# Attention and mixture of experts over eight batches: a new first and last batch, and shorter expert sums on GpSimd

## What is computed

```
xn  = layernorm(x)
q, k, v = xn @ Wq.T, xn @ Wk.T, xn @ Wv.T
att = softmax((q @ k.T * tril) / sqrt(512)) @ v        # masked scores are 0, not -inf
g   = top 2 of softmax(xn @ Wg), normalised            # 8 experts
ffn = sum_e g[e] * (xn @ We[e] + be[e])
out = x + att + ffn
```

## Time and profile before

| what | us |
|---|---|
| median of 3 runs | 129.04 |
| lowest and highest run | 128.96, 131.56 |
| the profiled execution, its own time | 128.2 |
| its span in the trace | 126.4 |

### The profile page before, as it was taken

How to read it: one execution, slowest core, us unless ns; L and a number is a source line. 1 busy time by engine, 2 the same in 40 slices (tenths; PEclk the granted TensorE clock), 3 DMA queues, 4 the chain that set the end, 5 groups by cost and what they waited for, 6 DMA issues and landing times.

```text
span 126.4 us, 2983 instructions
## 1 busy us (share of the span) xinstructions
PE 117.3 (93%) x738; PEld 104.7 (83%) x738; DVE 111.4 (88%) x539; ACT 101.1 (80%) x339; POOL 92.5 (73%) x207
## 2 busy tenths in 40 slices
PE   4999589999999999999999999999999999999950
PEld 4877476998899988998999888998899889898940
DVE  0587998999999999999999999989999998979952
ACT  0746299989997999789987999799978999887620
POOL 7400338689977899699968997889869996858950
PEclk9999999999999999999999999999999999999996
DMA  3998000000200011000200020001100020000202
GB/s 96 295 313 210 1 3 5 0 3 3 83 0 5 3 39 44 0 0 8 83 3 0 0 83 5 3 3 37 48 0 0 5 83 0 3 0 15 76 0 83
DMA packets 9249, 5.18 MB, mean 41 GB/s; under 512 B 392, under 2 KB 9104, under 8 KB 9232
## 3 DMA queue, kind: packets, MB, share of 16 engines
q1 hardware_dynamic: 8656, 4.66, 13.4%
q10 hardware_dynamic: 576, 0.33, 0.9%
HBM read 2.89 MB, written 2.10 MB: 39 GB/s over the span
## 4 chain that ended last, share of the span: by engine, by line
PE 83%; DVE 7%; DMA 2%; issue 2%; ACT 1%; POOL 1%; ACTq 1%; DVEq 0%; POOLq 0%
PE attb L307 14%; PE ring L250 13%; PE ring L246 13%; PE ring L247 12%; PE score L291 7%; PE score L247 4%; PE score L250 4%; PE score L246 3%; PE ring L316 3%; DMA wqk_s<-in_w_attention_dram 2%; PE ring L326 2%; PE score L357 2%; PE attb L350 1%; PE ring L327 1%; PE ring L329 1%
## 5 line engine op out<-in xcount | busy, mean ns | idle before, releaser
L911 ACT ACTIVATE ysc<-ring,gate 128x128 f32<-128x128 f32 x124 | 35.3, 375 | 1.8 <-PE ring L250 1.8
L246 PE MATMUL ring<-w_hi,xT_hi 128*128 128x512 f32 (+2 forms) x96 | 34.7, 361 | 0.2 <-ACT xT_hi L992 0.2
L250 PE MATMUL ring<-w_hi,xT_lo 128*128 128x512 f32 (+2 forms) x96 | 32.7, 341 | 0.0
L247 PE MATMUL ring<-w_lo,xT_hi 128*128 128x512 f32 (+2 forms) x96 | 32.5, 338 | 0.0
L1099 POOL TENSOR_TENSOR ysc<-ysc 128x256 f32<-128x256 f32 x31 | 22.8, 737 | 8.6 <-ACT ysc L911 8.6
L307 PE MATMUL attb<-c_s,probT 128*128 128x128 f32 x160 | 23.6, 278 | 0.8 <-ACT probT L945 0.8
L307 PEld LDWEIGHTS attb<-c_s,probT 128*128 128x128 f32 x160 | 21.6, 192 | 2.2 <-ACT probT L945 1.1
L558 DVE SCALAR_TENSOR_TENSOR mix<-ring,gate,mix 128x128 f32<-128x128 f32 x64 | 21.9, 345 | 0.5
L246 PEld LDWEIGHTS ring<-w_hi,xT_hi 128*128 128x128 f32 x96 | 18.1, 189 | 2.8 <-ACT xT_hi L992 0.5
L930 ACT ACTIVATE prob<-score,nmx 128x128 f32<-128x128 f32 (+3 forms) x32 | 17.5, 550 | 2.5 <-DVE nmx L614 1.8
L247 PEld LDWEIGHTS ring<-w_lo,xT_hi 128*128 128x128 f32 x96 | 18.1, 189 | 1.7
(11 more groups left out here) (108 smaller groups left out, 255.6 us busy)
## 6 DMA issues: line engine op xcount, KB each, us to landing
x_all<-in_x_dram SPq DMA_DIRECT2D x7, 256.0 KB, 5.5
out_dram<-o_s SPq DMA_DIRECT2D x7, 256.0 KB, 2.4
w_f<-in_w_stacked_dram SPq DMA_DIRECT2D x1, 256.0 KB, 5.1
w_f<-in_w_stacked_dram SPq DMA_DIRECT2D x1, 192.0 KB, 3.8
w_f<-in_w_stacked_dram SPq DMA_DIRECT2D x1, 132.0 KB, 2.8
x_all<-in_x_dram ACTq DMA_DIRECT2D x1, 128.0 KB, 2.9
x_all<-in_x_dram SPq DMA_DIRECT2D x1, 128.0 KB, 2.6
wqk_s<-in_w_attention_dram ACTq DMA_DIRECT2D x1, 128.0 KB, 3.0
```

What stands on the lines that cost most here:

```text
L246: nc.tensor.matmul(dst, hi, w_h, start=True, stop=False)
L247: nc.tensor.matmul(dst, hi, w_l, start=False, stop=False)
L250: return nc.tensor.matmul(dst, lo, w_h, start=False, stop=True)
L911: last = nc.scalar.mul(ysc[:, t, e, :], bank(f"A{t}", b)[:, e * P:(e + 1) * P], gate[:, b % 2, t, e:e + 1])
```

## The change

Everything else than what follows is as before; batches 1 to 6 keep their order.

- First batch. `expert_biases`, `biases_hi` and VectorE's `bias_rhs` are gone. The host now lays the biases out over 128 rows (`be_rows`), one DMA of 64.5 KB brings them in place of two, and GpSimd makes the rows: a rounding copy, a multiplication by a column, four additions over 32 partitions each. The first `sv_rows` waits for them (`be_ready`).
- GpSimd also makes `w_lo` of piece A (128 x 512), after VectorE has normalised batch 0. ScalarE casts `w_hi` of piece A after `xT_hi` instead of ahead of it.
- VectorE takes the four statistics of batch 1 in one go ahead of `u_lo`.
- The products of the identity are 6 and 4 pairs instead of 5 and 6.
- SyncE issues the load of batch 1 (and, behind it, of batches 2 to 7) only when the weights of piece B have landed.
- TensorE, VectorE and ScalarE get new lists for the first and the last batch. In the last, ScalarE copies the transposed probabilities of tile 3 ahead of `rows_copy`, not behind it, and TensorE transposes them one product (A3) earlier.
- In all batches `sum_experts` takes three operations instead of four: y7 lies in a fourth slot of `mix`, and y7 and the B experts are added in one operation of 128 x 256. `scale_last_act` in the last batch now waits for all expert sums of the batch before.

```diff
-WARM = (5, 6)
+WARM = (6, 4)
...
             sp.dma_start(w_f[:, a_cols], w_stacked[:, a_cols]).then_inc(S["w_a"], 16)
+            sp.wait_ge(S["w_b"], 16)
             sp.dma_start(x_all[:, NT * P:2 * NT * P].rearrange("p (t d) -> p t d", d=P), x_v[1]).then_inc(S["x1"], 16)
...
                 if t == 0:
                     dve.wait_ge(S["svh_ready"], b + 1)
+                    if b == 0:
+
+                        dve.wait_ge(S["be_ready"], 1)
...
             def scale_last_act(b):
 
                 act.wait_ge(S["gate_ready"], b + 1)
-                act.wait_ge(S["ffn_ready"], (b - 2) * NT + NT)
+                act.wait_ge(S["ffn_ready"], b * NT)
...
                 chain.step(nc.gpsimd.tensor_tensor(y[:, 0:2, :], y[:, 0:2, :], y[:, 2:4, :], ALU.add))
-                chain.step(nc.gpsimd.tensor_tensor(y[:, 0, :], y[:, 0, :], y[:, 1, :], ALU.add))
                 pool.wait_ge(S["y7_ready"], b + 1)
-                chain.step(nc.gpsimd.tensor_tensor(y[:, 0, :], y[:, 0, :], y7[:, b % 2, t, :], ALU.add))
                 pool.wait_ge(S["mix_ready"], b * NT + t + 1)
+                chain.step(nc.gpsimd.tensor_tensor(y[:, 0:2, :], y[:, 0:2, :], mix[:, t, 2:4, :], ALU.add))
                 if b > 1:
                     pool.wait_ge(S["fin_done"], (b - 2) * NT + t + 1)
-                nc.gpsimd.tensor_tensor(ffn[:, b % 2, t, :], y[:, 0, :], mix[:, t, 2, :], ALU.add
+                nc.gpsimd.tensor_tensor(ffn[:, b % 2, t, :], y[:, 0, :], y[:, 1, :], ALU.add
                                         ).then_inc(S["ffn_ready"], 1)
...
+            def bias_rhs():
+
+                pool.wait_ge(S["w_be"], 16)
+                chain.step(nc.gpsimd.tensor_copy(be_hi[:], be_s[:, 0:P]))
+                chain.step(nc.gpsimd.tensor_scalar(be_hi[:].bitcast(F32), be_hi[:].bitcast(F32), be_s[:, P:P + 1], None, ALU.mult))
+                for t in range(NT):
+                    r = slice(t * ROWS, (t + 1) * ROWS)
+                    chain.step(nc.gpsimd.tensor_tensor(rhs_rows[r, t, :], be_s[r, 0:P], be_hi[r, :].bitcast(F32), ALU.add))
+                pool.sem_inc(S["be_ready"], 1)
...
-            chain.step(nc.gpsimd.memset(rhs_rows[:].bitcast(F32), 0.0))
-            pool.sem_inc(S["consts_ready"], 1)
+            nc.gpsimd.memset(rhs_rows[:].bitcast(F32), 0.0)
             normal_rstd(0)
+
+            pool.wait_ge(S["xn0_ready"], NT)
+            pool.wait_ge(S["wa_ready"], 1)
+            nc.gpsimd.tensor_tensor(w_lo[:, a_cols], w_f[:, a_cols], w_hi[:, a_cols].bitcast(F32), ALU.subtract
+                                    ).then_inc(S["wla_ready"], 1)
+            bias_rhs()
```

More of the change, by code:

```diff
@@ L79, in step, with build @@
         self.need(self.mark(instruction))
-def build(nc, x, w_attention, w_stacked, be, shapes, out):
+def build(nc, x, w_attention, w_stacked, be_rows, out):
     B, T, D = x.shape
-    E = be.shape[0]
+    E = (w_stacked.shape[1] - P) // (P + 1)
     NT = T // P
@@ L380, in _ @@
             wide(0, "C", 0)
-            expert_biases(0)
+            project_u(0)
             wide(0, "C", 1)
-            project_u(0)
             wide(0, "C", 2)
             wide(0, "C", 3)
-            value_sums(0)
             scores(0, 0)
             scores(0, 1)
+            value_sums(0)
+            wide(0, "B", 0)
+            wide(0, "A", 0)
+            transpose_probs(0, 0)
             scores(0, 2)
-            transpose_probs(0, 0)
-            wide(0, "A", 0)
-            wide(0, "B", 0)
+            scores(0, 3)
+            transpose_x(1)
+            attend(0, 0)
             wide(0, "A", 1)
-            attend(0, 0)
-            transpose_x(1)
-            scores(0, 3)
             wide(0, "B", 1)
             wide(1, "C", 0)
-            project_u(1)
             transpose_probs(0, 1)
             wide(1, "C", 1)
+            project_u(1)
             wide(1, "C", 2)
@@ L447, in _ @@
             transpose_rows(B - 2)
+            value_sums(B - 1)
             attend(B - 2, 3)
@@ L450, in _ @@
             bias(B - 2)
-            wide(B - 1, "A", 0)
             scores(B - 1, 2)
             wide(B - 1, "B", 0)
+            wide(B - 1, "A", 0)
             wide(B - 1, "A", 1)
+            scores(B - 1, 3)
             wide(B - 1, "B", 1)
-            scores(B - 1, 3)
             wide(B - 1, "B", 2)
@@ L459, in _ @@
             wide(B - 1, "A", 2)
+            transpose_probs(B - 1, 2)
+            wide(B - 1, "B", 3)
             attend(B - 1, 0)
-            wide(B - 1, "B", 3)
-            transpose_probs(B - 1, 2)
+            transpose_probs(B - 1, 3)
             wide(B - 1, "A", 3)
             attend(B - 1, 1)
-            transpose_probs(B - 1, 3)
             attend(B - 1, 2)
@@ L753, in _ @@
             mix_b(0, 0, 1)
+            mask_scores(0, 1)
             mix_b(0, 0, 2)
+            negate_max(0, 1)
             x_lo(1)
```

147 lines of the change are left out of this document (59 added, 88 removed).

## The result

| | before | changed |
|---|---|---|
| median (4 runs each, same chip) | 129.0 us | 125.19 us |
| lowest and highest | 128.7, 131.56 | 124.7, 125.94 |
| profiled execution, its span | 128.2, 126.4 | 125.6, 123.9 |

A forecast was written before the change was run, and what follows sets the result against it. TensorE, busy 14.00 of 14.00 us, was taken to bound the loop, leaving gains only at start and end. 1.7 + 0 + 0.84 = 2.5 us off 129.04 gave 126.5 us, range 125.6 to 128.2.

The forecast's parts named there:

- the start's gain: First batch: `normalize(1)` starts at 14.6 instead of 16.33, and the last product of the first list moves equally: 1.7 us.
- chain 1: First batch, GpSimd: transposes, casts, weight split until 10.0, bias rows until 13.2, `rstd` and `nmr` 1.29, `normalize(1)` at 14.6.
- T0: First batch: TensorE's first transposes, forecast to start at 6.75 us; 7.55 in the profile before.
- T0 to N: First batch: from the first transposes, forecast at 6.75, to the start of `normalize(1)`, forecast at 14.6.
- Chain 2: First batch, VectorE and ScalarE: exponential of tile 0 at 12.7, its transpose and copy until 14.0, 0.6 us to spare.
- Rival 3: First batch: GpSimd operations are cheap (under 0.3 each), so the VectorE and ScalarE chain decides; 125.9 us; chance 0.20.
- Rival 1: Start's gain given back: GpSimd's rows cost 0.82 each, or batch 1's load takes 5.5 us; 128.0 us; chance 0.20.
- Rival 4: First batch: seven x loads served side by side, batch 1 lands at 13.7, VectorE stands still; 130.4 us; chance 0.04.
- the rule that I had cited: Load of batch 1: DMA engines take a ring's descriptors in order, so it is in time; without this 1.3 us more.
- The loop: Batches 1 to 6: GpSimd's sum falls from 2.12 to 1.94 per tile, but TensorE waits for nothing, so worth 0.
- The end: Last batch: copying tile 3's probabilities ahead of `rows_copy` removes TensorE's wait of 0.84 us.
- rival 2: Last batch: ScalarE waits for batch 6's sums, tile 3's exponential comes over 0.8 late; 127.3 us; chance 0.16.

The follow-up runs named there:

- experiment 12: Changed kernel without SyncE's wait for weight piece B ahead of the load of batch 1: 125.01 us, ratio 0.9741.
- experiments 2 and 6: 2: changed kernel with the four-operation sum put back, 126.52 us, ratio 0.9877; 6: kernel before with the three-operation sums alone, 127.8 us, ratio 0.9949.
- experiment 9: Kernel before with four small VectorE operations per batch given one SBUF input instead of two (values differ): 129.0 us, ratio 0.9985.
- experiment 10: Kernel before with only the pair sums made a one-input reduction: 128.77 us, ratio 1.0.
- experiment 5: Changed kernel with only ScalarE's last two copies exchanged back, `rows_copy` ahead of tile 3's probabilities: 125.95 us, ratio 0.985.
- experiment 3: Changed kernel with the last batch's TensorE, VectorE and ScalarE lists of the kernel before, the wait for batch 6's sums kept: 125.61 us, ratio 0.9801.
- experiment 7: Changed kernel with VectorE's pair sums (128x3) moved behind `u_lo` in the first batch: 124.7 us, ratio 0.9763.
- the anchor: The changed kernel run once more, unaltered, against the kernel before: 124.66 us, ratio 0.9733.

## Why the prediction was right, and where it was not

**The place and the kind of the start's gain: right; its size in the profile: 0.72, not 1.7.** The chain was the one named: GpSimd, with VectorE's chain shorter. The terms of chain 1:

- T0 at 6.75 (forecast) came at 7.46. Four identity products fewer gave 0.86 between a and T0 (0.85 forecast). But a was 5.17 instead of 4.40, since the attention weights landed 3.8 us after their issue, not 3.0; that is the whole 0.77. Column a spreads like this in both codes (4.38 to 5.17 in ten profiles of changed kernels, 4.40 to 5.02 in four of before), so I take it for chance.
- T0 to N: forecast 14.6 - 6.75 = 7.85, measured 8.14 (8.06 to 8.20 in the eight profiles with this order). In the rows above it is 2.14 to the start of the split (forecast 2.05), 1.28 for the split (1.17), 3.32 for the bias rows until `rstd` starts (3.2), 1.40 for `rstd` and `nmr` (1.4). Three of the four terms were a little short, by 0.3 together.

With the landing of before, this step comes to 0.86 + 0.64 - 0.01 = 1.5 us. Chain 2 came out nearly right by luck: the exponential of tile 0 stood 6.10 behind T0 (forecast 5.95), although the small addition booked at 0.1 took 0.86; the other terms had been too large by 0.6 together. Rival 3 fell: the GpSimd operations were not cheap, though the copy alone was (0.28). Rival 1 fell too: the load of batch 1 was there for its first statistic, at 9.84. Rival 4 fell with it: the seven loads took 4.4 in the median, and experiment 12 shows that the wait moves nothing. Whether a ring is served in order, the rule that I had cited, no run here shows.

**The loop: wrong.** The step that failed is "TensorE waits for nothing there, so this is worth 0", on the row that gave TensorE 14.00 of 14.00 us. It was worth 0.86 between X1 and X7 (experiments 2 and 6). TensorE does pause, once per batch, ahead of `transpose_x`. Before:

```profile
71.77 0.34 PE L247 MATMUL score<-xT_lo,uT_hi 128*128 128x384 f32 x1
71.95 0.34 PE L250 MATMUL score<-xT_hi,uT_lo 128*128 128x384 f32 x1
72.24 0.63 PE L316 MATMUL ring<-ident,xn 128*128 128x128 f32 x4
72.70 0.27 PE L291 MATMUL score<-ident,prob 128*128 128x128 f32 x1
```

And in the changed kernel:

```profile
70.68 0.34 PE L247 MATMUL score<-xT_lo,uT_hi 128*128 128x384 f32 x1
70.85 0.34 PE L250 MATMUL score<-xT_hi,uT_lo 128*128 128x384 f32 x1
71.03 0.61 PE L313 MATMUL ring<-ident,xn 128*128 128x128 f32 x4
71.47 0.27 PE L291 MATMUL score<-ident,prob 128*128 128x128 f32 x1
```

The start after a product of this size comes 0.18 us later when nothing is missing (71.77 to 71.95); before, the transposes came 0.29 later. From one set of transposes to the next it was 13.22, 13.69, 13.60, 13.61, 13.62, 13.67 us before and is 13.26, 13.51, 13.41, 13.45, 13.44, 13.48 now: nothing gained in the first period, into which the new first list still reaches, and 0.16 to 0.19 in each of the other five. Of that the pause is 0.11 to 0.12, the transposes themselves 0.02; the rest is spread in hundredths. The modelled end of the product (0.34 from its start) covers the pause, and so the busy time reads full. The Trainium skill ("Perfetto Trace Analysis", "Identifying the Most-Contended Engine") says that matmul busy time is a poor measure of how near TensorE is to its limit, and names the busy share of the weight loads, beside the share of peak arithmetic, as a better one. The trace agrees: with 14.00 in both, the weight loads rose from 12.67 to 12.90. What would have shown the pause beforehand is the spacing of starts.

Behind the pause stands this chain. VectorE and GpSimd before:

```profile
67.05 0.38 DVE L624 TENSOR_TENSOR tot<-em,masked_keys 128x4 f32<-128x4 f32 x1
...
68.86 0.17 DVE L490 TENSOR_SCALAR veps<-mv 128x4 f32<-128x4 f32 x1
```

```profile
66.95 0.46 POOL L1102 TENSOR_TENSOR ysc<-ysc,y 128x128 f32<-128x128 f32 x1
...
69.11 1.02 POOL L1085 TENSOR_TENSOR rstd<-veps,half 128x4 f32<-128x4 f32 x1
```

And in the changed kernel:

```profile
65.99 0.15 DVE L614 TENSOR_TENSOR tot<-em,masked_keys 128x4 f32<-128x4 f32 x1
...
67.57 0.17 DVE L480 TENSOR_SCALAR veps<-mv 128x4 f32<-128x4 f32 x1
```

```profile
65.37 0.74 POOL L1069 TENSOR_TENSOR ysc<-ysc,mix 128x256 f32<-128x256 f32 x1
...
67.82 1.02 POOL L1052 TENSOR_TENSOR rstd<-veps,half 128x4 f32<-128x4 f32 x1 [0.16 <-DVE veps L480]
```

`tot` ends when the GpSimd operation beside it ends (67.43 and 67.41; 66.14 and 66.11), and with the shorter sum that is 0.23 us after less waiting. From the start of `tot` to that of `veps` it is 1.81 before, 1.58 now: the same 0.23. `rstd` waits for `veps`, `normalize` for `rstd`, TensorE for `normalize`. Of these 0.23 TensorE could use the 0.11 of its pause before it was full. But GpSimd's own rows ahead of `rstd` ended at 68.95 before, 0.08 ahead of `veps`, and are sooner by as much now. How the gain divides between GpSimd's own shorter chain and VectorE's shorter wait stays open: experiment 9 was to part them and didn't, because its `tot` still waited. That the pair sums have no share is shown (experiment 10).

**The end: right in size, and for one more reason than given.** Forecast 0.84, measured 0.92; experiment 5 shows the wait of 0.84 come and go with the exchange, experiment 3 that the lists are worth 0.94. `bias` stayed hidden behind `attend`. VectorE has no slack left, though: its last product ahead of the finish (`mix<-c_s,gate,mix`, L575) took 0.74 beside a sum of GpSimd, 0.35 before, and ran until 120.31, where `bias` ended at 120.24 and the finish began at 120.28; before, the finish waited 1.46 for `bias`. What the prediction booked at nothing, the sums, is needed here too: with four operations only 0.41 of the 0.92 is left (26.87 - 26.46), since GpSimd's rows come late. This is rival 2's kind of loss, at another place than the one I had named; the wait that I had pointed at, ScalarE's for the sums of batch 6, was there (0.49 us) and hidden.

**The total.** In the profile 1.7 + 0 + 0.84 was forecast and 0.72 + 0.86 + 0.92 came: the sums agree because a late landing hid as much as the loop brought. Against the median the forecast was 1.3 us too slow, which is more than its range allowed for below (0.9). The loop's 0.86 is the larger part. The rest isn't shown; a start that is faster in most executions of the changed kernel than in its profiled one (below) would fit.

## What to carry to other kernels

A TensorE that reads 100% busy can still pause; before booking an edit at 0, compare the spacing of the starts around the steps that wait for other engines. An operation of 128x4 on VectorE can last until the GpSimd operation beside it ends, so cutting a GpSimd chain can shorten VectorE's too, and a long VectorE operation is worth shortening only if nothing is waited for right behind it. And cut two profiles into stretches before comparing their sums: a right total can be two wrong terms.

## What the hardware showed that I had not expected

**Small VectorE operations wait for the running GpSimd operation to end.** The same addition of 128x3 took 0.15 us with no GpSimd operation beside it and 0.86 beside the split of 128x512 (10.04 to 10.90; the split ran from 9.60 to 10.88), 0.61 beside a sum of 128x256 in the four-operation kernel:

```profile
61.37 0.61 DVE L671 TENSOR_TENSOR xs<-xs 128x3 f32<-128x3 f32 x1
```

```profile
61.23 0.73 POOL L1066 TENSOR_TENSOR ysc<-ysc 128x256 f32<-128x256 f32 x1
```

It goes the other way too. With the bias rows first, GpSimd's copy began beside a VectorE split and took 0.75 instead of 0.28:

```profile
7.43 0.75 POOL L1104 CAST be_hi<-be_s 128x128 fp32r<-128x128 f32 x1 [1.22 <-DVE xn L692]
7.48 0.55 DVE L485 TENSOR_TENSOR w_lo<-w_f,w_hi 128x384 fp32r<-128x384 f32 x1
```

Held up were operations of two SBUF inputs and two of one input and a constant (`tot` and `below` of experiment 9); not held up were the reduction (experiment 9), the negation of the row maximum (128x1, 0.13 to 0.16 us in all profiles) and operations that read PSUM (the products of `mix` with a bank, 315 to 354 ns wherever they fell before). The Trainium skill ("SBUF — State Buffer", "Who interferes with whom") says that VectorE and GpSimd share a pair of SBUF ports as an exclusive lock for a whole instruction, that VectorE needs it for two SBUF inputs and can for copies, casts and operations with a scalar, and never for a reduction. On two inputs, on a scalar and on the reduction the traces agree, with the numbers above; VectorE has no copy or cast in these kernels. On one thing they differ: VectorE's product for `gate` (two SBUF inputs) ran in its usual 0.19 inside GpSimd's `rstd` of 1.02 us, 92 times in the fourteen profiles, and in experiment 7 the addition took 0.15 (10.56 to 10.71) inside GpSimd's multiplication by a column (10.25 to 10.86). So not every GpSimd instruction holds VectorE off from start to end. The kernel before:

```profile
69.62 0.19 DVE L543 TENSOR_TENSOR gate<-gexp,grec 128x32 f32<-128x32 f32 x1
```

**TensorE doubles its pace early in the kernel, and not always at the same time.** Eight products of the identity took, start to next start, 0.213 us each in the first profile of the changed kernel and 0.112 in the second (5.41 on), with nothing changed; the granted clock reads 1.00 in both. Later in the kernel such a product takes about 0.11 as well. That ratio of nearly two is that of the levels 1.2 and 2.4 GHz. TensorE had worked from 1.66 us on in both, with a pause of 0.58 and of 0.44 ahead of a. The anchor:

```profile
5.03 0.54 PE L359 MATMUL score<-wqk_s 128*128 128x128 f32 x2 [0.44 <-DMA wqk_s<-in_w_attention_dram]
5.41 1.06 PE L354 MATMUL score<-ident 128*128 128x128 f32 x8
6.50 0.58 PE L364 MATMUL ring<-ident,xn 128*128 128x128 f32 x2
```

The slow pace throughout stands in three of the four profiles with the old pairs (a to T0 3.14 or 3.15) and in three of the ten with the new ones (2.29 or 2.30); it costs up to 0.96 us (2.29 against 1.33), and what it does to T0 passes one to one into N. At the fast pace the identity products are no longer what holds T0: in the anchor the transposes then waited 0.2 us for VectorE's first normalised tile (6.10 to 6.45), and T0 was 6.50 although a was as late as 5.03. So a late landing of the attention weights cost its whole length at the slow pace, and next to nothing at the fast one: experiment 3, with a at 4.38, had T0 at 6.46. This is why a single profile can misjudge the start by most of what was to be measured there. What sets the moment wasn't tried and stays open.
